# Another order of TensorE's work inside the period of a self-attention stage

## What is computed

```python
for l in range(N_LAYERS):
    h = rmsnorm(x, n1[l])
    qkv = h @ Wqkv[l].T + bqkv[l]
    q, k, v = jnp.split(qkv, 3, axis=-1)
    q = apply_rope(split_heads(q, H), cos, sin)
    k = apply_rope(split_heads(k, H), cos, sin)
    v = split_heads(v, H)
    o = merge_heads(sdpa(q, k, v, causal_bias)) @ Wo[l].T + bo[l]
    x = x + o
```

## Times and profile before

| | us |
|---|---|
| median of 3 runs | 2164.78 |
| lowest, highest | 2158.61, 2176.61 |
| the profiled execution, its own time | 2163.22 |
| its span, first to last instruction | 2161.5 |
| mean granted TensorE clock of its span | 0.917 |

### The profile page before, as it was taken

One profiled execution on the slowest core, in us unless ns is written; L12 is line 12 of the kernel. 1 busy time (PEld: TensorE's weight loads), 2 busy tenths in 40 slices (PEclk: granted clock), 3 DMA queues, 4 the chain that ended last, 5 costly groups with the idle time before them and its releaser, 6 DMA issues.

```text
span 2161.5 us, 34224 instructions
## 1 busy us (share of the span) xinstructions
PE 1847.2 (85%) x12747; PEld 1122.3 (52%) x12747; DVE 1450.1 (67%) x3531; ACT 1068.2 (49%) x1519; POOL 666.2 (31%) x903
## 2 busy tenths in 40 slices
PE   5978998594777888898989998989999998989966
PEld 4556665373544444565544564644455554456543
DVE  8667765643677777864577784567786467787468
ACT  2655665131453465564456566266656346656510
POOL 3121102503534353310455320255330245431030
PEclk9989998586796898999899999999999979999978
DMA  6342333121000000141000033000014000004100
GB/s 221 104 137 97 106 104 92 47 82 38 20 1 13 1 1 13 34 104 46 15 1 1 3 90 80 28 1 1 1 51 116 6 15 1 2 21 103 49 0 20
DMA packets 80745, 100.88 MB, mean 47 GB/s; under 512 B 31462, under 2 KB 46190, under 8 KB 79940
## 3 DMA queue, kind: packets, MB, share of 16 engines
q1 hardware_dynamic: 78532, 94.50, 15.4%
q0 software_dynamic: 2048, 4.20, 0.7%
HBM read 52.43 MB, written 12.38 MB: 30 GB/s over the span
## 4 chain that ended last, share of the span: by engine, by line
PE 41%; DVE 15%; ACT 6%; issue 4%; POOL 1%; SPq 1%; DMA 1%; DVEq 0%; POOLq 0%; ACTq 0%
PE wide L822 29%; PE acc L822 11%; DVE maxima L1747 6%; ACT prob L1989 2%; DVE hid L1251 1%; DMA masked_q<-q_g 1%; DVE x L1808 1%; ACT prob L1912 1%; DVE qkv L1715 1%; DVE moments L1294 1%; SPq L746 1%; DVE hid L1418 1%; DVE hn L1339 1%; ACT hn L1877 1%; POOL rstd L2051 1%
## 5 line engine op out<-in xcount | busy, mean ns | idle before, releaser
L1747 DVE TENSOR_REDUCE maxima<-wide 128x2 f32<-128x512 f32 (+3 forms) x512 | 406.5, 819 | 159.3 <-PE wide L822 156.7
L1989 ACT ACTIVATE prob<-wide 128x768 f32<-128x768 f32 (+1 forms) x384 | 332.6, 881 | 160.1 <-PE wide L822 159.6
L1912 ACT ACTIVATE prob<-wide 77x1024 f32<-77x1024 f32 x256 | 258.0, 1017 | 99.0 <-PE wide L822 98.9
L822 PE MATMUL wide<-q_g 32*128 32x256 f32 (+3 forms) x2048 | 274.7, 405 | 35.0 <-ACT prob L1989 16.8
L2215 POOL TENSOR_SCALAR_AFFINE_SELECT prob<-prob 128x256 f32<-128x256 f32 (+1 forms) x384 | 186.9, 491 | 352.9 <-ACT prob L1989 350.5
L1427 DVE TENSOR_REDUCE maxima<-wide 128x8 f32<-128x616 f32 x256 | 203.0, 796 | 118.6 <-PE wide L822 117.2
L822 PEld LDWEIGHTS wide<-q_g 32*128 32x128 f32 x2048 | 144.3, 196 | 212.2 <-issue 101.2
L2051 POOL TENSOR_TENSOR rstd<-moments,cst 128x4 f32<-128x4 f32 x88 | 89.8, 1020 | 522.0 <-DVE moments L1315 277.6
L1833 ACT ACTIVATE q_g<-wide 128x1024 fp32r<-128x1024 f32 x128 | 131.1, 1024 | 184.4 <-PE wide L822 184.4
L1833 ACT ACTIVATE q_g<-acc 128x512 fp32r<-128x512 f32 x192 | 114.5, 596 | 170.0 <-PE acc L822 169.6
L822 PE MATMUL wide<-kx,q_g 128*128 128x312 f32 x512 | 179.8, 417 | 7.7 <-DVE maxima L1427 4.7
(11 more groups left out here) (243 smaller groups left out, 3006.8 us busy)
## 6 DMA issues: line engine op xcount, KB each, us to landing
masked_q<-q_g SPq DMA_DIRECT2D x448, 64.0 KB
masked_q<-mask_l SPq DMA_DIRECT2D x84, 308.0 KB
masked_k<-kx SPq DMA_DIRECT2D x224, 19.5 KB, 2.3
A<-in_w SPq DMA_DIRECT2D x2, 2048.0 KB, 12.9
unit_w<-in_unit_w SPq DMA_DIRECT2D x8, 448.0 KB, 3.7
ffn_w<-in_ffn_w SPq DMA_DIRECT2D x4, 768.0 KB, 4.4
slots_in<-v_third SPq DMA_DIRECT2D x1, 2560.0 KB, 13.6
prob<-slots_in SPq DMA_DIRECT2D x8, 320.0 KB, 3.1
```

The lines of the kernel that those rows point to most:

```text
L822: return e.matmul(out, lhsT, rhs, start=start, stop=stop, is_transpose=turn)
L1747: e.tensor_reduce(top[:, t, h], v[:, :, at0:at0 + P * t + P], AX.X, ALU.max, negate=True).then_inc(*made("max", *([("free", tile)] if t == ...
L1912: e.activation(p[0:SC, :], s[0:SC, :], ACT.Exp, bias=0.0, scale=1.0).then_inc(*made("exp", pb, ("free", tile)))
L1989: e.activation(pv, sv, ACT.Exp, bias=0.0, scale=8 ** -0.5).then_inc(*made("exp", pb, ("free", tile)))
```

## The change

Only the order of steps in `self_steps` is edited, not what any step does. `attend` runs its logits in another order (h0 = 0 before h0 = 2) and two rows later, and gives its values step 0 to `finish`. FULL goes from row 1, behind C0, to row 3, behind C1. `finish` has values steps 0 and 1 together in row 4, and 2 and 3 together in row 10. `o_turn` and `o_norm` go from the end of `finish` to row 3 of the next period, and `out_turn` and `out_project` to rows 5 and 9, behind C2 and C4, in `bring_out`, which takes the place of `project_out`. `turn` goes from row 0 to row 2, behind C0.

```diff
     def project_in(b):
-        return in_rows((0, ("turn", "s", l, b)), (4, ("qkv", l, b, 0)), (8, ("qkv", l, b, 1)))
+        return in_rows((2, ("turn", "s", l, b)), (4, ("qkv", l, b, 0)), (8, ("qkv", l, b, 1)))
...
     def attend(b, g):
         logits = lambda j, h0: ("self_logits", l, b, g, j, h0)
-        return in_rows((1, ("self_full", l, b, g)), (4, logits(0, 2)), (6, logits(0, 0)), (8, logits(1, 2)),
-                       (10, logits(1, 0)), (12, ("self_values", l, b, g, 0)))
+        return in_rows((3, ("self_full", l, b, g)), (6, logits(0, 0)), (8, logits(0, 2)), (10, logits(1, 0)), (12, logits(1, 2)))
...
         if (b, g) == (B - 1, G - 1):
 
-            s = [(0, logits(2)), (0, logits(0)), (1, values(1)), (2, values(2)), (2, values(3))]
+            s = [(0, logits(0)), (0, logits(2)), (1, values(0)), (1, values(1)), (2, values(2)), (2, values(3))]
...
-        s = [(0, logits(2)), (2, logits(0)), (4, values(1)), (8, values(2)), (10, values(3))]
-        if g % 2:
-            s += [(11, ("o_out", "s", l, b, g // 2)), (13, ("o_turn", "s", l, b, g // 2)), (13, ("o_norm", "s", l, b, g // 2))]
-        return in_rows(*s)
-
-    def project_out(b):
-        return in_rows((4, ("out_turn", "s", l, b)), (8, ("out_project", "s", l, b)))
-
-    items = [[prepare(b, g), scores(b, g), attend(b, g), finish(b, g)] + ([project_out(b)] if g == G - 1 and b + 1 < B else [])
-             for b in range(B) for g in range(G)]
+        s = [(2, logits(0)), (4, values(0)), (4, values(1)), (4, logits(2)), (10, values(2)), (10, values(3))]
+        return in_rows(*s, *([(12, ("o_out", "s", l, b, g // 2))] if g % 2 else []))
+
+
+    def bring_out(b, g):
+        s = [(3, ("o_turn", "s", l, b, g // 2)), (3, ("o_norm", "s", l, b, g // 2))]
+        return in_rows(*s, *([(5, ("out_turn", "s", l, b)), (9, ("out_project", "s", l, b))] if g == G - 1 else []))
+
+    items = [[prepare(b, g), scores(b, g), attend(b, g), finish(b, g)] for b in range(B) for g in range(G)]
+    for n in range(1, B * G - 2, 2):
+        items[n + 2][2] = beside(items[n + 2][2], bring_out(*divmod(n, G)))
```

## The result

The changed kernel takes 2211.0 us (median of 4 runs, 2209.36 to 2212.62) against 2167.0 for the kernel before beside it (4 runs, 2158.61 to 2176.61). The ratio is 1.0204, with a 95% interval of 1.0166 to 1.0242. The forecast was 2176 with a range to 2204: the sign of the likeliest case was right, and its size was too small by a factor of about four.

What follows compares the result with a forecast made beforehand. TensorE (41% of the chain) was to bound it, with waits for VectorE and ScalarE reading its buffers. Three stages gave +11 us, the first 0: 2163.2 became 2174, then 2176 as the runs' median; range 2134 to 2204.

Steps and rivals of the forecast that it cites:

- the quiet period: Head-group period with no other work, between C5's masks: from 9.67 to about 10.2 us, +0.55.
- The idle time at L(2,0): The other logits pair after C5's mask waits about 0.7 us for C5's buffer, starting at 1.64 us.
- lost cover: Values step 0 no longer hides C5's reduction: C5's mask to C2's mask 4.87 us against 4.52, +0.35.
- the quiet 0.17 us: FULL's wait for C5's reduction and two small operations in a period without other work; claimed to go.
- the held-up case: FULL's longer wait where GpSimd delays VectorE's first small operation, 1.04 us instead of 0.18; claimed mostly gone.
- the periods with other work: Periods also holding projections, turns or rotations: one batch of four +1.1 us, all terms +3.7 per stage.
- rotations +0.1: Periods after the two first rotations of q and k: claimed 0.1 us longer.
- out_turn +0.2: Period with `out_turn` behind C2's mask: buffer ring shifts, C3 waits for C2's reduction, +0.2 us in all.
- out_project and cut_k -0.3: `out_project` behind C4's reduction, its adds and `cut_k` later; FULL's long wait mostly fits under C1: -0.3 us.
- Faster: Rival: no wait at L(2,0), FULL's waits and switches gained; 2110 us at most, about 2140 by half; chance 0.22.
- Clearly slower: Rival: every period loses what the quiet one does, GpSimd still holding VectorE up; 2203 to 2209 us; chance 0.19.
- Switches saved: 168 fewer TensorE tiling changes in the four stages, 0.09 to 0.14 us each: 15 to 24 us of demand.

Runs made afterwards that it cites:

- step 0 back: Changed kernel with values step 0 alone put back behind C5, values otherwise as changed: 2154.36 us, ratio 0.9939.
- the hidden filler: Changed kernel with six extra pairs of mask matmuls in each C0 tile: 2186.44 us, ratio 1.0127; with three pairs 2199.29 us.
- short GpSimd operations: Changed kernel with GpSimd's rotation products and sums and output-projection bias addition cut short in layers 2 to 4: 2189.97 us, ratio 1.0131.

## Why the prediction was wrong

**Right in size: the quiet period.** It was forecast at 10.2 us from m5 to m5 and is 10.12 in the third stage and 10.29 in the second and fourth. The idle time at L(2,0) came as forecast (1.60 us behind m5, for 1.64). But its cost was read wrongly: with step 0 back, and no such idle time, the period is 10.08, so leaving step 0's place costs 0.04 us, and 0.21 where GpSimd's triangle holds up VectorE. The other 0.4 us come with the edits that stay in that kernel: FULL's new place alone makes 9.98 of 9.66 (m5 to m2 4.83 for 4.52), with the logits' order it is 10.16 (m2 to m5 5.41 for 5.15). The +0.35 that the sum put on lost cover was a number that fitted by way of another step, by luck.

**Wrong: "Behind C1 it asks later than that, so the quiet 0.17 us goes, and so does most of the held-up case."** This is the step of the order that failed. Two edits move FULL in opposite directions: C1 and a pair of logits come ahead of it, and values step 0 goes away from ahead of it. By start times TensorE asks for FULL 1.73 us behind m5 before (m0 at 1.59 in the earlier trace rows, and 0.14 from a mask to FULL) and 2.12 after: only 0.4 us later. Where the small operation takes 0.83 in place of 0.18, FULL is ready at 2.83. With step 0 kept it asks at 2.99, later than the hold of such a period. In the four stages FULL's waits are 33.2 us before (the prediction counted 36, with two stages taken like the third), 15.8 in the changed kernel, 1.7 with step 0 back, 0.2 with FULL and logits alone on the kernel before: the cover that was taken away and the wait that was to go were in the same place, and they were counted apart.

**Too small: the periods with other work.** From m5 to m5, forecast and measured (with `turn`, second full batch: 14.47 before, 15.01 in the kernel with the hidden filler): `turn` +1.1, measured +0.5 (+0.9 against the one period of 14.14 before); rotations +0.1, measured +0.53; out_turn +0.2, measured +0.65; out_project and cut_k -0.3, measured +0.56 and +0.33; the quiet one with `o_turn` +0.9, measured +0.82; the last out_project period -0.5, measured +0.05; the last period nothing, measured +0.91. With the quiet period these sum to +3.2 forecast and +6.9 measured in a stage. The terms of the rotations, of `out_project` with `cut_k` and of the last period rested on FULL's wait being gone or on nothing changing: with short GpSimd operations these periods are 10.11, 11.19, 10.77 and 12.68 us, 0.6 to 1.3 shorter. That of `out_turn` failed otherwise, since FULL waits there neither before nor after and short operations leave it at 12.43; the rows have 0.44 us idle at L(2,0) and 0.36 at C3 there, each for a reduction of VectorE. In the first batch one period got shorter (9.23 against 10.25), others can't be compared at full clock.

**Put at nothing: the granted clock.** This is the second step that failed, and between the two profiles the larger. The sum took stages 2 to 4 at full clock on both sides and nothing outside them, and no sentence of it says why the clock should stay. At 0.35 us for each us at 1.2 GHz the account is:

| | us |
|---|---|
| stages 2 to 4, order: (578.8 - 26.5) - (548.2 - 19.1) | +23.2 |
| stages 2 to 4, clock: 21.2 x 0.35 | +7.4 |
| unedited stretches, clock: 49.8 x 0.35 | +17.4 |
| unedited stretches, rest | +5.7 |
| first stage and all ahead of it | -4.3 |
| sum | +49.4 |

The forecast for this was +11. Twelve us of the miss are the order (7.7 per stage for 3.7), 25 are the clock. This pair probably overstates the clock, since 0.902 is the lowest of the changed kernel's ten runs (up to 0.919). The mean over six runs of the changed kernel beside the fillers is 0.910, against 0.918 over eleven of the kernel before beside them. That is 44 us more at 1.2 GHz, 13 to 15 us of the 45 by which they differ. That the clock costs this much in the stages is shown by the fillers. For the unedited stretches only the correlations, over the profiles and over the runs of the kernel before, are shown: no experiment touched them alone. The first of them has 23.9, 23.9, 23.9 and 20.5 us at 1.2 GHz in the four profiles of the changed order, with and without filler, and 6.8 before and with step 0 back, so there it goes with the order ahead of it; the others differ between two profiles of the changed kernel itself (end of the program 245.0 with 54.6 and 239.2 with 44.6). Why the clock falls there stays open. The start of the program, unedited too, differs by up to 10 us between kernels and was not explained.

**The rivals.** "Faster" had its condition right (L(2,0) under 1.2 us behind m5) and it wasn't met. "Clearly slower" named the right mechanism, GpSimd's operations holding VectorE up where FULL now stands, and its 2203 to 2209 came within 8 us. In part that was luck, as it had no clock in it and took the same 0.6 us in every period. It had 19 chances in 100, though the rows of FULL, of the mask and of the values step gave the moment at which TensorE would ask to 0.1 us. Switches saved: the pair of values takes 1.64 us, where steps 0 and 1 apart take 0.99 and 0.78, so the 0.1 us of a switch is there; no run here gained time from it.

## What to carry to other kernels

When an edit takes work away from ahead of a waiting instruction and another pushes that instruction back, work out the one number that matters, when the engine now asks, with both edits together; here it was 0.4 us where 1.3 were on offer. Work that stands where the engine would else idle can hide its whole length. Moving such work away, to join it to its like and save a tenth of a microsecond of switching, cost 2.6% here (2211 against 2154 us), and 5.7% in the kernel before. And idle time on TensorE can be paid for twice, once as itself and once in the granted clock: filling it gave 22.6 us back. Give the clock a term of its own before a forecast sums at full clock; in the kernel before, whose runs have mean clocks from 0.908 to 0.929, the times are spread over 36 us.

## What the runs showed of the hardware

Filler matmuls in idle time made a kernel faster: 768 more small matmuls (12 in each of 64 periods), 22.6 us less. One us at 1.2 GHz cost 0.30 to 0.38 us here, in stages and in stretches with other work alike. VectorE's operation of 16 columns takes 0.18 us alone. If it starts while GpSimd is inside an addition, product or subtraction of 512 columns (1.05 to 1.28 us), it ends 0.04 us after that one ends, whenever it began: so in all 215 cases in the stages of the 17 profiles, in which it took 0.55 to 1.28 us. With GpSimd's products cut to 64 columns it takes 0.18 in the period shown. Beside GpSimd's triangles (0.41 to 0.64 us) it took over 0.3 us in 23 of 279 cases.
